# Reordering the opening of a one-core token-mixing, projection and LoRA kernel, and moving its wave generation from GpSimd to ScalarE

## The chip, the cores and the metric

The kernel runs on one core of one Trainium2 chip. The metric is the device time of one execution in microseconds (us). The engines go by short names here as in the profile: PE is TensorE (matrix products and transposes through the identity), DVE is VectorE, ACT is ScalarE, POOL is GpSimd, and SP is the engine whose queue issues nearly all DMAs.

## The reference

What is computed, cut to what matters (L = 1024, H = 128 heads of rows, C = 32, N = 64 states):

```python
K = 2.0 * einsum('chn,hnl->chl', Cc * (exp(dtA) - 1) / A, exp(dtA * ell)).real   # S4D kernel, (32, 128, 1024)
h = K
h = h + (layernorm(h) @ W1.T + b1)                     # W1 is 1024 x 1024
n = layernorm(h)
gates = softmax(n @ Wr.T)                              # 4 experts
lora = sum_e gates_e * 2.0 * (n @ A_e.T) @ Bm_e        # rank 8 each
h = h + (n @ W2.T + b2) + lora                         # W2 is 1024 x 1024
```

## The kernel before, in words

The 4096 rows are worked in 16 tiles t of 8 heads, each in two halves i of 128 rows. One half (t, i) passes through these stages.

- **Waves and S4 product.** `phases` makes the turns of a tile (step times frequency, plus a quarter for the cosine), `round_turns` (DVE, L960 and L963) leaves the fraction, `sines` (ACT, L666, between two table loads) takes the sine, `decays` the exponential, and `make_u` (DVE, L970) multiplies the two. `make_m` (DVE, three passes, L994 and L997) makes the other factor from x, which PE turned (`turn_x`) and ACT copied (`copy_x`). `s4(t, i)` is 64 small PE products into the two banks `ps_a`.
- **First layer norm and G1.** `keep_h` (DVE, L1003) stores h and its sum, `square_1` and `rstd_guess` (ACT), `normalise_1` (DVE, L1028). The result is split in two f16 parts, `high_1` (ACT, L692) and `low_1` (DVE, L1034). `turn_x1` has SP transpose both by DMA into `x1`. `attn(t, i)` is the product G1 with W1: for each of 8 blocks k three partial products (hi by hi, hi by lo, lo by hi) over two halves of the columns, 48 matmuls into the two banks `ps_g1`.
- **Second layer norm and G2.** `keep_h2` (DVE, L1042) reads `ps_g1`, then `square_2`, `normalise_2`, `high_2`, `low_2`, `turn_x2` in the same manner. `project` makes the LoRA and gate products, `ffn_part` is the product G2 with W2 into `ps_g2`, `gate_begin`, `gate_exp`, `gate_end` make the gates, `turn_lora` and `copy_lora` turn them, `ffn_end` adds the LoRA part, and `finish` writes the result for `store`.

In the loop the order on PE is `turn_x(t+1)`, and then twice `s4(after)`, `attn(t, i)`, `project`, `ffn_part`, `turn_lora`, `ffn_part`, `ffn_end` of the half before. The order of the work is written out by hand on each engine, with semaphores between them; an engine runs its list strictly in order. ACT starts an iteration with `copy_x(t+1)`. POOL makes in each iteration one product for the phases and one for the exponents, each over 128x1024 elements (`wave`, L843), when `round_turns` and `make_u` of the tile before are done; ACT then adds the quarter (`quarters`, L657) and takes the exponential (L662) with one instruction each.

**Before the loop** the weights must be made ready. Both are scaled by a power of two, found from a bound on their norm: PE multiplies each 128-row block with itself (`square_attn`, `square_ffn`, L449; `square_lora_a` adds the LoRA weights), DVE reads the diagonal (`weight_norms`, L1113, L1119), POOL takes the largest over the partitions, and DVE makes the scale (`split_scales`, L1126 to L1135). W1, blocks 0 to 7, is turned on PE (`turn_weight`, L473) and split by ACT (`attn_hi`, L710) and DVE (`attn_lo`, L1142) out of PSUM. W2, blocks 8 to 15, is split first (`ffn_hi` L721, `ffn_lo` L1150) and then transposed by DMA (`turn_weights` on SP). `high` parts are announced on `s_whi`, `low` parts on `s_wlo`, counters whose order the tuple `SPLITS` holds.

The prologue on PE interleaves all this with the first halves: `attn(0, 0)` by column halves as the blocks of W1 come, `s4(0, 1)`, `attn(0, 1)`, `turn_lora_b`, `s4(1, 0)`, `project(0, 0)`, G2 of (0, 0). G2 there waits at once for all eight blocks of W2 (`s_wf`).

Of the kernel before, what the change touches and what calls it, by code (L numbers as in the profile page):

```python
# [15 lines left out]
P = 128  # L16
# [6 lines left out]
HT = 8  # L23
# [23 lines left out]
SPLITS = (0, 1, 2, 3, 8, 4, 9, 5, 6, 10, 7, 11, 12, 13, 14, 15)  # L47
# [13 lines left out]
def program(nc, x, log_dt, B, inv_A_real, A_imag, attn_w, attn_b, ffn_w, ffn_b, lora_a, lora_b,  # L61
            gate_w, out):
    with ExitStack() as ctx:
# [26 lines left out]
        norms = sb("norms", [P, 4])  # L90
# [35 lines left out]
        x2_tok = stage[:, KB - 2, :]  # L126
# [4 lines left out]
        def x1_part(part):  # L131
            return x1[:, :].bitcast(F16).rearrange("p (s k t) -> p s k t", s=2, k=KB)[:, part, :, :]
# [28 lines left out]
        s_norm = sem("weight_squares_summed")  # L161
        s_diag = sem("weight_norms_read")
# [3 lines left out]
        s_wf, s_wf_0 = sem("ffn_weight_transposed"), sem("first_ffn_rows_transposed")  # L166
# [13 lines left out]
        s_phase = sem("phase_ready")  # L180
        s_arg = sem("exponent_ready")
# [130 lines left out]
        def _(sp):  # L312
# [92 lines left out]
        def _(pe):  # L405
# [82 lines left out]
            def ffn_part(t, i, ks):  # L488
# [93 lines left out]
            pe.wait_ge(s_wf, 32 * (KB - 1))  # L582
            ffn_part(0, 0, range(0, 6))
# [712 lines left out]
```

## Time and profile before

| | |
|---|---|
| median of 3 runs | 863.32 us (862.34 to 863.69) |
| time of the profiled execution | 863.63 us |
| its span, first to last instruction | 861.8 us |
| PE busy | 822.8 us (95% of the span) |
| DVE busy | 602.3 us (70%) |
| ACT busy | 323.6 us (38%) |
| POOL busy | 67.2 us (8%) |
| mean granted TensorE clock | 0.99 |

The span lies 1.8 us under the time of the same execution. The page shows one execution; the queries used here give, for a stretch of it, the instructions in order of time (start, duration, and in square brackets the idle time before them and what ended it), the waits summed by who waited for whom, and groups of instructions with their mean duration.

### The profile page before, as it was taken

What the parts mean: (1) busy time and instruction counts of PE and PEld (TensorE: products, weight loads), DVE (VectorE), ACT (ScalarE), POOL (GpSimd) and SP (SyncE); (2) the same over time, 40 slices, a digit from 0 to 9 for tenths busy, and PEclk for the clock granted to TensorE, in tenths of its full rate; (3) what the DMA queues carried; (4) which work ended last, traced back from release to release, by engine and by line L of the source; (5) the groups of instructions that cost most, each with busy time, mean ns of one, the idle gap of its engine ahead of it and who ended that gap; (6) DMA issues with size and microseconds to landing.
All of it is one profiled execution on the core that took longest, in us unless ns stands there. A gap on an engine that the chain in (4) does not pass through costs nothing.

```text
span 861.8 us, 15882 instructions
## 1 busy us (share of the span) xinstructions
PE 822.8 (95%) x6162; PEld 437.5 (51%) x6162; DVE 602.3 (70%) x1150; ACT 323.6 (38%) x543; POOL 67.2 (8%) x38
## 2 busy tenths in 40 slices
PE   6976979999999999999999999999999999999998
PEld 6863434545545454545545454545545454545543
DVE  6867877587777767687777767687776757687433
ACT  4645544252524334252424334252424334252210
POOL 0001002020200102020200102020200202000000
PEclk9988999999999999999999999999999999999999
DMA  8536643223332333223323333223323333223323
GB/s 293 154 75 112 115 84 77 58 65 73 73 68 66 73 84 75 50 67 72 79 61 73 73 81 73 52 61 72 85 56 79 73 79 66 62 53 69 75 50 73
DMA packets 175267, 68.47 MB, mean 79 GB/s; under 512 B 160456, under 2 KB 168776, under 8 KB 175248
## 3 DMA queue, kind: packets, MB, share of 16 engines
q1 hardware_dynamic: 175152, 68.09, 36.0%
q8 instruction: 11, 0.18, 0.1%
q10 hardware_dynamic: 96, 0.13, 0.0%
q14 instruction: 8, 0.07, 0.0%
HBM read 13.67 MB, written 16.78 MB: 35 GB/s over the span
## 4 chain that ended last, share of the span: by engine, by line
PE 61%; DVE 18%; ACT 10%; issue 10%; DMA 0%; DVEq 0%; SPq 0%; ACTq 0%
PE ps_g L495 24%; PE ps_g L435 21%; PE ps_a L427 7%; DVE y L1028 2%; DVE m_im L994 2%; DVE h_tok L1042 2%; ACT junk L678 2%; DVE h_tok L1003 2%; ACT L666 2%; ACT x_tok L692 2%; PE ps_g L506 2%; ACT turn_u L666 2%; PE ps_g L619 1%; DVE stat L1014 1%; PE ps_x L449 1%
## 5 line engine op out<-in xcount | busy, mean ns | idle before, releaser
L435 PE MATMUL ps_g<-wa_hi,x 128*128 128x512 f16 x1024 | 272.7, 382 | 8.5 <-DVE wa_lo L1142 4.8
L495 PE MATMUL ps_g<-wf_hi,x 128*128 128x512 f16 x992 | 264.9, 380 | 0.0
L435 PEld LDWEIGHTS ps_g<-wa_hi,x 128*128 128x128 f16 x1024 | 98.3, 98 | 130.2 <-issue 9.4
L435 PE MATMUL ps_g<-wa_lo,x 128*128 128x512 f16 x512 | 155.0, 382 | 0.0
L495 PEld LDWEIGHTS ps_g<-wf_hi,x 128*128 128x128 f16 x992 | 95.5, 98 | 105.0 <-issue 1.3
L495 PE MATMUL ps_g<-wf_lo,x 128*128 128x512 f16 x496 | 148.0, 380 | 0.0
L672 ACT ACTIVATE junk<-ps_a,stat 128x1024 bf16<-128x1024 f32 x32 | 35.7, 1115 | 150.9 <-DVE stat L1006 150.9
L1104 DVE SCALAR_TENSOR_TENSOR result<-ps_g,unscale,h_tok 128x1024 f32<-128x1024 f32 x31 | 39.8, 1284 | 68.5 <-PE ps_g L506 68.5
L843 POOL TENSOR_TENSOR phase<-z_turn,steps_b 128x1024 f32<-128x1024 f32 x14 | 38.1, 2719 | 576.6 <-DVE turn_u L963 576.6
L435 PEld LDWEIGHTS ps_g<-wa_lo,x 128*128 128x128 f16 x512 | 50.4, 98 | 61.0 <-issue 1.8
L495 PEld LDWEIGHTS ps_g<-wf_lo,x 128*128 128x128 f16 x496 | 48.6, 98 | 59.2 <-issue 1.1
L678 ACT ACTIVATE junk<-h_tok,stat 128x1024 bf16<-128x1024 f32 x32 | 36.7, 1148 | 106.0 <-DVE stat L1046 106.0
L692 ACT ACTIVATE x_tok<-y 128x1024 f16<-128x1024 f32 x32 | 33.8, 1057 | 100.0 <-DVE y L1028 100.0
L427 PE MATMUL ps_a<-turn_u,m 128*32 128x128 f32 x2048 | 64.2, 279 | 5.3 <-DVE wa_lo L1142 4.2
L427 PEld LDWEIGHTS ps_a<-turn_u,m 128*32 128x32 f32 x2048 | 55.3, 112 | 13.6 <-issue 5.9
L1003 DVE SCALAR_TENSOR_TENSOR h_tok<-ps_a,bias_bc 128x1024 f32<-128x1024 f32 x32 | 39.2, 1224 | 25.2 <-PE ps_a L427 25.2
L1042 DVE SCALAR_TENSOR_TENSOR h_tok<-ps_g,unscale,h_tok 128x1024 f32<-128x1024 f32 x32 | 40.9, 1278 | 20.7 <-PE ps_g L435 20.7
L1034 DVE TENSOR_TENSOR x_tok<-y,x_tok 128x1024 f16<-128x1024 f32 x32 | 39.1, 1222 | 21.5 <-ACT x_tok L692 21.5
L698 ACT ACTIVATE stage<-xn 128x1024 f16<-128x1024 f32 x32 | 33.8, 1057 | 47.6 <-DVE xn L1053 47.6
L1059 DVE TENSOR_TENSOR stage<-xn,stage 128x1024 f16<-128x1024 f32 x32 | 39.2, 1225 | 12.7 <-ACT stage L698 12.6
L1028 DVE TENSOR_SCALAR y<-ps_a,stat 128x1024 f32<-128x1024 f32 x32 | 43.0, 1343 | 1.2
L994 DVE TENSOR_TENSOR m<-x_t,q 128x1024 f32<-128x1024 f32 x32 | 40.7, 1271 | 1.6
(194 smaller groups left out, 832.8 us busy)
## 6 DMA issues: line engine op xcount, KB each, us to landing
out<-result SPq DMA_DIRECT2D x124, 128.0 KB, 2.1
x_raw<-in_x SPq DMA_DIRECT2D x64, 64.0 KB
stage<-in_L_ffn_W SPq DMA_DIRECT2D x8, 512.0 KB, 9.9
h_tok<-in_L_attn_weight SPq DMA_DIRECT2D x2, 512.0 KB, 4.6
x<-in_L_attn_weight SPq DMA_DIRECT2D x2, 512.0 KB, 7.0
result<-in_L_attn_weight SPq DMA_DIRECT2D x2, 512.0 KB, 8.3
x<-x_tok SPq DMA_TRANSPOSE x64, 3.2
x<-stage SPq DMA_TRANSPOSE x64, 3.2
```

Of the source, the lines that this page charges most:

```text
L427: mm = pe.matmul(ps_a[q * C:(q + 1) * C, a // 4, (a % 4) * P:(a % 4 + 1) * P], m[:, i, q, a * C:(a + 1) * C], u[:, HS * i + q, :], start=T ...
L435: mm = pe.matmul(ps_g1[:, o, :], x1_part(part)[:, k, :], ws[:, k, o * HALF:(o + 1) * HALF], start=k == 0 and part == 0 and ws is wa_hi, st ...
L495: pe.matmul(ps_g2[:, o, :], xs[:, k, :], ws[:, k, o * HALF:(o + 1) * HALF], start=k == 0 and xs is x2_hi and ws is wf_hi, stop=False)
L678: act.activation(junk[:, :], h2_tok[:, i, :], ACT.Square, bias=stat_2[:, 1:2], accum_out=stat_2[:, 2:3]).then_inc(s_ssq2, 1)
L692: act.activation(by_token(x1_tok[:, :], 0), y[:, :], ACT.Copy).then_inc(s_hi1, 1)
L994: dve.tensor_tensor(dst.rearrange("p h (a c) -> p h a c", a=KB), c, f, ALU.mult)\
L1003: dve.scalar_tensor_tensor(out=h_tok[:, i, :], in0=whole(ps_a), scalar=1.0, in1=bias_bc[:, :], op0=ALU.mult, op1=ALU.add, accum_out=stat_1 ...
L1028: dve.tensor_scalar(y[:, :], whole(ps_a), stat_1[:, 1:2], stat_1[:, 7:8], ALU.add, ALU.mult).then_inc(s_xn1, 1)
L1034: dve.tensor_tensor(by_token(x1_tok[:, :], 1), y[:, :], by_token(x1_tok[:, :], 0), ALU.subtract)\
L1042: dve.scalar_tensor_tensor(out=h2_tok[:, i, :], in0=whole(ps_g1), scalar=unscale[:, 0:1], in1=h_tok[:, i, :], op0=ALU.mult, op1=ALU.add, a ...
L1059: dve.tensor_tensor(by_token(x2_tok, 1), xn[:, :], by_token(x2_tok, 0), ALU.subtract)\
L1104: dve.scalar_tensor_tensor(out=result[:, i, :], in0=whole(ps_g2), scalar=unscale[:, 1:2], in1=h2_tok[:, i, :], op0=ALU.mult, op1=ALU.add). ...
```

## The change

The sums of squares of W2's blocks 12 to 15 are taken by ACT, one row sum for each (`square_rows`, the bound is then a maximum over the diagonal of the other four blocks and these four columns of `norms`), and no longer by PE. W1's splits come ahead of most of W2's: `attn_lo(2, 3)` stands before the second `weight_norms`, and the orders of high and low parts differ (`SPLITS`, `LOWS`). Piece 4 of W1 is turned into `ps_g2` instead of `ps_a`. The product G1 of half (0, 1) goes into `ps_g2`, with its x in `x2[:, 1]`, so that it needs neither `ps_g1` nor `x1`; `turn_lora_b` goes into `ps_g1`. G2 of (0, 0) is made by column halves, the first of which waits for blocks 8 to 11 only, with `s4(1, 0)` inside it. Copies 9 and 10 of W2's splits lie in `result`, and `x2_tok` in `stage[:, 0]`. In all tiles the waves are made by ACT: `phases` and `decays` are 8 instructions each over 128x128 elements, with the scale addressed by a register in the loop, at the top of the iteration; POOL's `wave`, ACT's `quarters` and the one-instruction `decays` are gone.

The diff, cut to its core:

```diff
-SPLITS = (0, 1, 2, 3, 8, 4, 9, 5, 6, 10, 7, 11, 12, 13, 14, 15)
+SPLITS = (0, 1, 2, 3, 4, 5, 8, 6, 9, 7, 10, 11, 12, 13, 14, 15)
+LOWS = (0, 1, 2, 3, 4, 5, 8, 6, 7, 9, 10, 11, 12, 13, 14, 15)
-        norms = sb("norms", [P, 4])
+        norms = sb("norms", [P, 8])
-        x2_tok = stage[:, KB - 2, :]
+        x2_tok = stage[:, 0, :]
-            ps = (ps_g1, ps_g2, ps_g1, ps_g2, ps_a, None, ps_g2, None)[n]
+            ps = (ps_g1, ps_g2, ps_g1, ps_g2, ps_g2, None, ps_g2, None)[n]
...
@@ sync
             def turn_x1(t, i):
-                at_least(sp, s_g1, 2 * t + i)
+                first = (t, i) == (0, 1)
+                if first:
+                    sp.wait_ge(s_wt, 5)
+                else:
+                    at_least(sp, s_g1, 2 * t + i)
...
             turn_x1(0, 0)
             load_x(1)
-            turn_weights(KB, KB + 3)
+            turn_weights(KB, KB + 1)
             sp.wait_ge(s_wt, KB)
             load_lora_a(wg_rows, s_wg)
-            turn_weights(KB + 3, KB + 4)
             turn_x1(0, 1)
-            turn_weights(KB + 4, 2 * KB)
+            turn_weights(KB + 1, KB + 5)
             turn_x2(0, 0)
+            turn_weights(KB + 5, 2 * KB)
             load_x(2)
@@ tensor
             s4(0, 0)
-            square_ffn(KB + 2, 2 * KB)
+            square_ffn(KB + 2, KB + 4)
             square_lora_a()
-            pe.wait_ge(s_wlo, split_done(0))
+            pe.wait_ge(s_wlo, low_done(0))
             turn_weight(2)
-            pe.wait_ge(s_wlo, split_done(1))
+            pe.wait_ge(s_wlo, low_done(1))
             turn_weight(3)
-            pe.wait_ge(s_xn1, 1)
+            pe.wait_ge(s_wlo, low_done(3))
             turn_weight(4)
             pe.wait_ge(s_diag, 2)
             turn_weight(5)
+            pe.wait_ge(s_wlo, low_done(4))
+            turn_weight(6)
             pe.wait_ge(s_x1, 32)
-            pe.wait_ge(s_wlo, split_done(3))
-            attn_part(0, 0, range(0, 1), (0,))
-            turn_weight(6)
-            attn_part(0, 0, range(1, 5), (0,))
-            pe.wait_ge(s_wlo, split_done(4))
+            attn_part(0, 0, range(0, 4), (0,))
             s4(0, 1)
-            attn_part(0, 0, range(5, KB), (0,))
-            pe.wait_ge(s_wlo, split_done(5))
+            pe.wait_ge(s_wlo, low_done(5))
             turn_weight(7)
-            pe.wait_ge(s_wlo, split_done(7))
+            attn_part(0, 0, range(4, KB), (0,))
+            pe.wait_ge(s_wlo, low_done(7))
             attn_part(0, 0, range(KB), (1,)).then_inc(s_g1, 1)
             turn_x(1)
             turn_lora_a()
-            attn(0, 1)
+            pe.wait_ge(s_x1, 64)
+            attn_part(0, 1, range(0, 6), ps=ps_g2)
             turn_lora_b()
-            s4(1, 0)
+            attn_part(0, 1, range(6, KB), ps=ps_g2).then_inc(s_g1, 1)
...
             project(0, 0)
             pe.wait_ge(s_lb_sb, 2)
             pe.wait_ge(s_wf_0, 32)
-            pe.wait_ge(s_wf, 32 * (KB - 1))
-            ffn_part(0, 0, range(0, 6))
+            pe.wait_ge(s_wf[0], 96)
+            pe.wait_ge(s_h2, 2)
+            ffn_part(0, 0, range(0, 3), (0,))
+            s4(1, 0)
+            ffn_part(0, 0, range(3, KB), (0,))
+            pe.wait_ge(s_wf[1], 128)
+            ffn_part(0, 0, range(0, 3), (1,))
             turn_lora(0, 0)
-            ffn_part(0, 0, range(6, KB))
+            ffn_part(0, 0, range(3, KB), (1,))
             ffn_end(0, 0)
@@ scalar
             def phases(T):
+                at_least(act, s_frac, T)
                 for k in range(HT):
                     a = act.activation(phase[:, k, :], steps_b[:, :], ACT.Identity,
-                                       scale=z_turn[:, T * HT + k:T * HT + k + 1], bias=quarter[:, :])
+                                       scale=z_turn[:, bass.ds(T * HT + k, 1)], bias=quarter[:, :])
+            def decays(T):
+                act.wait_ge(s_u, T)
                 for k in range(HT):
+                    a = act.activation(decay[:, k, :], steps_b[:, :], ACT.Exp,
+                                       scale=z_re[:, bass.ds(T * HT + k, 1)])
+            def square_rows(*blocks):
+                for n in blocks:
+                    act.wait_ge(s_wload[n], 16)
+                    at_least(act, s_rows, n - KB - KB // 2)
+                    act.activation(junk[:, :], raw_block(n), ACT.Square,
+                                   accum_out=norms[:, n - KB:n - KB + 1]).then_inc(s_rows, 1)
             square_1(0, 0)
             rstd_guess(0, 0, stat_1, s_ssq1, s_log1, s_y1)
+            square_rows(12, 13)
             high_1(0, 0)
             attn_hi(2, 3)
+            square_rows(14, 15)
+            attn_hi(4, 5)
             ffn_hi(8)
-            attn_hi(4)
+            attn_hi(6)
             ffn_hi(9)
-            attn_hi(5, 6)
-            act.wait_ge(s_frac, 1)
-            phases(1)
+            attn_hi(7)
+            act.wait_ge(s_rows, KB // 2)
             square_1(0, 1)
...
             with act.Fori(1, TILES - 1) as t:
+                phases(t + 1)
+                decays(t + 1)
                 copy_x(t + 1)
@@ gpsimd
-            waves(2)
-            with pool.Fori(1, TILES - 2) as t:
-                waves(t + 2)
@@ vector
             low_1(0, 0)
+            attn_lo(2, 3)
             dve.wait_ge(s_lo1, 1)
             weight_norms(1, [ps_x[:, :], ps_p[:, :]])
-            attn_lo(2, 3)
+            make_first_u(1)
             split_scales(1)
+            attn_lo(4)
+            make_m(0, 1)
+            attn_lo(5)
             ffn_lo(8)
-            make_first_u(1)
-            make_m(0, 1)
-            attn_lo(4)
-            ffn_lo(9)
-            attn_lo(5)
+            attn_lo(6)
             keep_h(0, 1)
-            attn_lo(6)
-            ffn_lo(10)
             attn_lo(7)
             normalise_1(0, 1)
-            ffn_lo(11)
+            ffn_lo(9)
             low_1(0, 1)
-            round_turns(1)
-            ffn_lo(12)
-            dve.wait_ge(s_wf_0, 32)
-            keep_h2(0, 0)
+            ffn_lo(10, 11, 12)
             split_lora_b()
...
-            ffn_lo(13, 14)
+            ffn_lo(13)
+            keep_h2(0, 0)
+            ffn_lo(14)
+            round_turns(1)
             normalise_2(0, 0)
             ffn_lo(15)
             low_2(0, 0)
...
+            make_m(1, 0)
+            dve.wait_ge(s_wf_0, 32)
+            keep_h2(0, 1, ps_g2)
+            make_u(1)
+            gate_begin(0, 0)
+            gate_end(0, 0)
+            keep_h(1, 0)
+            normalise_2(0, 1)
+            normalise_1(1, 0)
+            copy_lora(0, 0)
+            low_1(1, 0)
             make_m(1, 1)
-            keep_h(1, 0)
-            normalise_1(1, 0)
-            low_1(1, 0)
-            gate_begin(0, 0)
-            keep_h2(0, 1)
-            gate_end(0, 0)
-            normalise_2(0, 1)
             low_2(0, 1)
-            copy_lora(0, 0)
```

## Rows read from the trace of the kernel before

**Rows 1.** The page: PE's granted clock in 40 slices of the span.

```profile
PEclk9988999999999999999999999999999999999999
```

**Rows 2.** Waits of PE, 0 to 121 us: sum, times, longest.

```profile
PE ps_p L500 <- DVE lora_split L1091: 4.8, 1, 4.8
PE ps_g L435 <- DVE wa_lo L1142: 4.8, 2, 3.6
PE ps_a L427 <- DVE wa_lo L1142: 4.2, 1, 4.2
PE ps_g L435 <- DMA x<-x_tok: 3.7, 1, 3.7
```

**Rows 3.** Waits of PE, 120 to 862 us.

```profile
PE ps_p L500 <- DVE lora_split L1091: 6.4, 13, 0.5
```

**Rows 4.** PE in order of time, prologue.

```profile
35.91 1.16 PE L449 MATMUL ps_x<-stage 128*128 128x128 f32 x8
...
46.82 1.16 PE L449 MATMUL ps_x<-x 36*128 36x128 f32 x8
...
62.26 3.64 PE L427 MATMUL ps_a<-turn_u,m 128*32 128x128 f32 x64 [4.23 <-DVE wa_lo L1142]
...
84.76 1.03 PE L435 MATMUL ps_g<-wa_hi,x 128*128 128x512 f16 x2 [3.65 <-DMA x<-x_tok]
...
121.09 1.95 PE L427 MATMUL ps_a<-turn_u,m 128*32 128x128 f32 x64
```

**Rows 5.** Groups on DVE, 34 to 121 us: busy, mean ns.

```profile
L1150 DVE SCALAR_TENSOR_TENSOR stage<-stage,scale 128x1024 f16<-128x1024 f32 x6 | 7.6, 1280 | 4.8 <-ACT stage L721 4.8
...
L997 DVE TENSOR_TENSOR m<-m,m_im 128x1024 f32<-128x1024 f32 x3 | 3.7, 1225 | 0.1
```

**Rows 6.** ACT in order of time, prologue.

```profile
42.19 1.06 ACT L692 ACTIVATE x_tok<-y 128x1024 f16<-128x1024 f32 x1 [2.80 <-DVE y L1028]
...
59.57 3.19 ACT L637 ACTIVATE phase<-steps_b,quarter,z_turn 128x128 f32<-128x128 f32 x8
...
81.03 2.43 ACT L651 ACTIVATE decay<-steps_b,z_re 128x128 f32<-128x128 f32 x8
...
84.19 1.15 ACT L678 ACTIVATE junk<-h_tok,stat 128x1024 bf16<-128x1024 f32 x1 [0.73 <-DVE stat L1046]
```

**Rows 7.** DVE in order of time, prologue.

```profile
54.16 0.14 DVE L1135 TENSOR_SCALAR unscale<-power 128x1 f32<-128x1 f32 x1
...
84.07 0.59 DVE L1165 TENSOR_SCALAR params<-params 128x256 f32<-128x256 f32 x1
...
85.88 0.22 DVE L1214 TENSOR_SCALAR lora_split<-ones,scale 128x2 fp32r<-128x2 f32 x1
...
103.64 1.22 DVE L1003 SCALAR_TENSOR_TENSOR h_tok<-ps_a,bias_bc 128x1024 f32<-128x1024 f32 x1
...
110.35 1.23 DVE L1034 TENSOR_TENSOR x_tok<-y,x_tok 128x1024 f16<-128x1024 f32 x1 [1.12 <-ACT x_tok L692]
```

**Rows 8.** SP's queue, prologue.

```profile
81.34 1.34 SPq L338 DMA_TRANSPOSE x<-x_tok  x1
```

**Rows 9.** One iteration of the loop: ACT in order of time.

```profile
503.64 1.06 ACT L698 ACTIVATE stage<-xn 128x1024 f16<-128x1024 f32 x1 [1.44 <-DVE xn L1053]
510.45 0.60 ACT L631 ACTIVATE x_t<-ps_x 128x512 f32<-128x512 f32 x1 [5.75 <-PE ps_x L413]
```

**Rows 10.** The same iteration: DVE.

```profile
513.88 1.23 DVE L994 TENSOR_TENSOR m<-x_t,q 128x1024 f32<-128x1024 f32 x1
...
523.27 2.26 DVE L970 TENSOR_TENSOR turn_u<-decay,turn_u 128x1024 f32<-128x1024 f32 x1 [0.58 <-ACT turn_u L666]
525.45 1.27 DVE L1042 SCALAR_TENSOR_TENSOR h_tok<-ps_g,unscale,h_tok 128x1024 f32<-128x1024 f32 x1
```

**Rows 11.** The same iteration: POOL.

```profile
521.74 2.71 POOL L843 TENSOR_TENSOR phase<-z_turn,steps_b 128x1024 f32<-128x1024 f32 x1 [42.79 <-DVE turn_u L963]
```

**Rows 12.** The same iteration: PE.

```profile
531.40 0.32 PE L500 MATMUL ps_p<-ident,lora_split 128*98 128x128 f32 x1 [0.49 <-DVE lora_split L1091]
```

More of the change, by code:

```diff
@@ L429, in s4, with attn_part @@
                 mm.then_inc(s_s4, 1)
-            def attn_part(t, i, ks, halves=(0, 1)):
+            def attn_part(t, i, ks, halves=(0, 1), ps=ps_g1):
                 for k in ks:
@@ L434, in attn_part @@
                         for o in halves:
-                            mm = pe.matmul(ps_g1[:, o, :], x1_part(part)[:, k, :], ws[:, k, o * HALF:(o + 1) * HALF],
+                            mm = pe.matmul(ps[:, o, :], x1_part(part, ps is ps_g2)[:, k, :], ws[:, k, o * HALF:(o + 1) * HALF],
                                            start=k == 0 and part == 0 and ws is wa_hi,
@@ L486, in project, with ffn_part @@
                 mm.then_inc(s_proj, 1)
-            def ffn_part(t, i, ks):
+            def ffn_part(t, i, ks, halves=(0, 1)):
                 if 0 in ks:
@@ L493, in ffn_part @@
                     for xs, ws in ((x2_hi, wf_hi), (x2_hi, wf_lo), (x2_lo, wf_hi)):
-                        for o in range(2):
+                        for o in halves:
                             pe.matmul(ps_g2[:, o, :], xs[:, k, :], ws[:, k, o * HALF:(o + 1) * HALF],
@@ L517, in turn_lora_b @@
                 pe.wait_ge(s_lbn, 3)
+                pe.wait_ge(s_h2, 1)
                 for o in range(2):
                     for j in range(4):
-                        mm = pe.transpose(ps_g2[0:KL, o, j * P:(j + 1) * P], lbn[:, 4 * o + j, :].bitcast(F32),
+                        mm = pe.transpose(ps_g1[0:KL, o, j * P:(j + 1) * P], lbn[:, 4 * o + j, :].bitcast(F32),
                                           ident[:, :])
@@ L772, in _ @@
             ffn_hi(10)
-            attn_hi(7)
             high_1(0, 1)
-            ffn_hi(11, 12)
+            ffn_hi(11, 12, 13)
+            phases(1)
             copy_x(1)
-            second_decays()
+            ffn_hi(14)
             square_2(0, 0)
             rstd_guess(0, 0, stat_2, s_ssq2, s_log2, s_y2)
-            ffn_hi(13, 14, 15)
-            act.wait_ge(s_wlo, split_done(14))
+            ffn_hi(15)
+            act.wait_ge(s_wlo, low_done(8))
             high_2(0, 0)
-            sines(1)
             act.wait_ge(s_wg_t, 1)
@@ L788, in _ @@
                 act.wait_ge(s_lbt, o + 1)
-                act.activation(lb[:, o * HALF:(o + 1) * HALF], ps_g2[0:KL, o, :], ACT.Copy).then_inc(s_lb_sb, 1)
+                act.activation(lb[:, o * HALF:(o + 1) * HALF], ps_g1[0:KL, o, :], ACT.Copy).then_inc(s_lb_sb, 1)
+            decays(1)
+            sines(1)
+            square_2(0, 1)
+            rstd_guess(0, 1, stat_2, s_ssq2, s_log2, s_y2)
+            gate_exp(0, 0)
             square_1(1, 0)
@@ L793, in _ @@
             high_1(1, 0)
-            gate_exp(0, 0)
-            square_2(0, 1)
-            rstd_guess(0, 1, stat_2, s_ssq2, s_log2, s_y2)
             high_2(0, 1)
@@ L1035, in low_1, with keep_h2 @@
                     .then_inc(s_lo1, 1)
-            def keep_h2(t, i):
+            def keep_h2(t, i, ps=ps_g1):
                 j = 2 * t + i
@@ L1041, in keep_h2 @@
                 at_least(dve, s_result, j - 1)
-                dve.scalar_tensor_tensor(out=h2_tok[:, i, :], in0=whole(ps_g1), scalar=unscale[:, 0:1],
+                dve.scalar_tensor_tensor(out=h2_tok[:, i, :], in0=whole(ps), scalar=unscale[:, 0:1],
                                          in1=h_tok[:, i, :], op0=ALU.mult, op1=ALU.add,
@@ L1112, in weight_norms @@
                     blocks = ps.shape[1] // P
+                    norm = 2 * k + j
                     a = dve.scalar_tensor_tensor(out=y[:, cols].rearrange("p (k o) -> p k o", o=P),
@@ L1219, in _ @@
             low_2(0, 0)
-            make_m(1, 0)
-            make_u(1)
             dve.wait_ge(s_wg_hi, 1)
```

71 lines of the change are left out of this document (29 added, 42 removed).

## The prediction

> **What bounds the kernel now.** I read the page first. The granted clock is full nearly everywhere but in the third to sixth slice of 40, all before 130 us [rows 1]. So I asked for PE's waits before and after 120 us. Before it, PE waits for W1's low parts, for the transposed x of half (0, 1), and at the end for the gates [rows 2]; the four kinds sum to 17.5 us, and with the waits of about 1 us it is 20. After it PE waits for one thing only, 13 times about 0.5 us, 6.4 us in all, for `lora_split` [rows 3]. Then I read PE, DVE, ACT and SP in order of time up to the start of `s4(1, 1)` at 121.09 [rows 4], from where on nothing but those short waits holds PE. The change has two sizes to find: how much sooner `s4(1, 1)` starts, and what an iteration of the loop gains or loses.
>
> **The opening, step by step.** Each wait is priced by the chain that now ends last. Full-width DVE passes take 1.23 to 1.28 us and follow each other every 1.2 [rows 5].
>
> 1. *Squares.* Six blocks of W2 take PE from 35.91 to 46.82, 1.82 each [rows 4]. Four go: 7.3 us, so the norm's sums end near 41.6 instead of 48.8. They don't set the next step. DVE now does `attn_lo(2, 3)` first, and these need ACT's `attn_hi(2, 3)`, which follow `high_1(0, 0)`. That one ends at 43.25 in any case [rows 6]: the two squares ahead of it (1.15 each and 0.1 for the sum, 2.5 together, by the square of rows 6) fill 2.5 of the 2.80 us in which ACT idles there. So high parts 2 and 3 end at 44.3 and 45.3, low ones at 45.7 and 46.9. The second pair of squares ends at 47.8, under this. Reading the diagonal takes DVE to 48.2, and with the maximum over the partitions the scale stands at 49.7, against 54.3 [rows 7]. That is 4.6 us sooner, not 7.3. If W2's blocks had not landed, ACT's squares would be late; PE read block 12 near 39.6 without a wait, so this costs nothing.
> 2. *DVE sets the pace to the second x.* From 49.7: low 4 (1.25), `make_m(0, 1)` (3 passes, 3.5), low 5 in two pieces (1.4), low 8 and low 6 (2.4) end at 58.2. PE has meanwhile turned pieces 4 to 6, begun G1 at 52 and ended `s4(0, 1)` at 56.5, so `keep_h(0, 1)` starts at 58.2. In the row of before that `s4` began at 62.26 and took 3.64 at half clock [rows 4]. From the start of `keep_h` to the end of `low_1` it takes 7.9 us where nothing comes between (103.64 to 111.58 [rows 7]); lows 7 and 9 fit in its waits. So `low_1(0, 1)` ends at 66.1. Its transpose lands 3.4 us after its issue (81.34, and PE starts at 84.76 [rows 4, 8]): x is there at 69.5, against 84.7. On SP this transpose now stands ahead of those of blocks 9 to 12.
> 3. *G1 of both halves.* PE ends the first by 66.4. The second needs no free `ps_g1`. With 48 matmuls (10.4) and `turn_lora_b` (1.05) it runs from 69.5 to 81.0.
> 4. *DVE again.* Between 66.1 and the end of `keep_h2(0, 1)`, which G2 of (0, 0) needs since it lies in `ps_g2`, DVE has 13 full-width passes (six `ffn_lo`, two `keep_h2`, one of `round_turns`, `low_2`, three of `make_m(1, 0)`), 15.6 us, and short ones: `split_lora_b` to `lora_split` 2.0 (84.07 to 86.10 [rows 7]), the passes of `round_turns` and `normalise_2` on SBUF alone 1.4, statistics and `wg_lo` 1.8. Sum 20.8, so 86.9. x2 of (0, 0), split by 81.6, lands at 85 to 86: the same time. ACT's phases (3.19) and exponentials (2.43 [rows 6]) lie in ACT's gaps here. G2 starts at 87.0.
> 5. *The price of PE's pause.* PE has little to do from 81.0 to 87.0. After the pauses of 4.23 and 3.65 us in rows 4, `s4` took 3.64 instead of 1.95 and the first matmuls of G1 ran at the lower of the two clock levels, 1.2 instead of 2.4 GHz. I take the first 9 matmuls and part of `s4(1, 0)` at half clock: 3.9 plus 2.1 instead of 1.95 plus 1.9. `s4(1, 0)` ends at 93.0. The same holds for the pause from 43.4 to 47.0 (PE waits for low 3): the transposes of pieces 4 and 5 are on the chain of step 2, and I take 0.6 us for it. Its bounds are nothing, and 3 us if the half clock lasts through `s4(0, 1)`.
> 6. *To the loop.* From the end of `s4(1, 0)`: 7.9 to the end of `low_1(1, 0)`, then `make_m(1, 1)` 3.5, on which `s4(1, 1)` waits: 104.5. PE itself is through with G2 (39 more matmuls, 8.4, and 1.4 for the small products) at 102.9. All eight blocks of W2 are needed at 96; SP issues the last at 90, and they land by 95.
>
> With the 0.6 of step 5 `s4(1, 1)` starts at 105.1 instead of 121.09: **16.0 us saved**. Bounds: 102.6 with no half clock anywhere gives 18.5 (the last step then starts at 90.9 and nothing is added); 3 us for the first pause, 2 more for the second, and half a microsecond of wait at each of four handovers give 11.
>
> **The loop.** DVE's `make_u` takes 2.26 us there, while POOL's product of the phases runs (521.74 to 524.45), and `keep_h2` stands right behind it [rows 10, 11]. The same kind of instruction takes 1.23 elsewhere [rows 5]. Without POOL, `make_u` ends 1.03 sooner, `keep_h2` starts as much sooner (its product ended at 522.5), and by the chain `keep_h2`, `square_2`, `normalise_2`, `gate_end` so does `lora_split`. PE's wait of 0.49 [rows 12] goes: **6.4 us saved** over the loop [rows 3]. More is not to be had: the rest of the iteration shows no idle time on PE.
>
> What ACT pays: per tile 3.19 and 2.43 instead of two instructions of about 1.1, so 3.4 more. They stand after `high_2`, which ends at 504.70, and end at 510.3; `copy_x` started at 510.45 after 5.75 idle [rows 9]. So the cover holds to 0.1 us, and behind `copy_x` waits `make_m` at 513.88 [rows 10], 2.8 us later. A register address costs something that no row of ACT shows. From below it is nothing, if it is made ready under the instruction before; from above I take 0.2 us each, the gap ahead of DVE's first register-addressed pass less the usual overlap (513.76 to 513.88 [rows 10], and about 0.1). 16 of them give 3.2 us. The slack is 2.8 and then the 0.54 that `make_u` gives beyond the wait: 3.4. So either end costs nothing, and I take nothing.
>
> The Trainium skill (VectorE: DVE Perf Modes, the section on the TRN2 errata) warns of this: operations out of SBUF pay a fixed time each, so small tiles cost more. The rows agree, 5.62 against 2.2 us for the same elements; it is ACT's time, which has that room. Its cycle formula gives 0.29 us for 128 elements, an estimate from that page: 4.7 for 16, and the sum would be the same by it.
>
> **Sum.** 16.0 + 6.4 = 22.4. The profiled execution took 863.63 us (span 861.8, 1.8 beside it), so 841.2; against the median of 863.32 it is 841 as well. I say 841.3.
>
> **The rivals.**
>
> - *The loop keeps its wait.* ACT's table loads and sine end at 524.5, and if `square_2` or the order of `copy_x` is pushed, the 1.03 us of `make_u` does not reach `lora_split`. For: the slack left is only 0.54. Against: the chain has no other wait of that size. Time: 863.6 - 16.0 = 847.6.
> - *The opening gives only what PE no longer does.* DVE is the bound from 49.7 on, and a wait that I have placed wrong (SP's transposes of eight blocks packed together, landing over 4 us late, or the clock) gives the rest back: 7.3 saved, and the loop's 6.4: 850. Against: the x of (0, 1) comes 15 us sooner by three independent queues.
> - *Slower: register-addressed ACT instructions.* In the loop each of the 16 pays x more. Beyond 0.21 us each, every microsecond reaches PE 14 times: 14 * 16 * (x - 0.21) over a loop without the wait. It decides at x = 0.31, where it eats all 22.4 us. At 0.35 the time is 841.3 + 31 = 873. For: no row of ACT has such an address. Against: DVE's shows 0.2 at most, and those behind the first show none.
> - *No change* would need the opening's gain to be lost before the loop; PE has nothing to wait on for that long.
>
> **How the numbers follow.** Forecast 0.58; loop keeps its wait 0.18; opening gives only 7.3 0.10; better than the sum (no half clock, 838 and below) 0.07; slower 0.05; no change 0.02. The range reaches from 838 (the bound of no half clock, 863.6 - 18.5 - 6.9) to 851 (just over the second rival). Faster by over 0.2% (1.7 us, about what a measurement here can tell from no change) 0.93, same 0.02, slower 0.05.
>
> **What would show each step.** In the profile after: the scale of W2 near 49.7; `low_1(0, 1)` ending near 66 and G1 of (0, 1) starting near 69.5; G2 of (0, 0) near 87 at half clock; `s4(1, 1)` near 105; in the loop `make_u` at 1.22 and no wait of PE for `lora_split`; ACT's 16 instructions in 5.6 us ending by 511 in the iteration of rows 9. The prediction is wrong if PE's waits in the loop grow (then ACT's instructions are over 0.6 us apart), or if DVE idles between 50 and 87, which would mean a wait that I have not seen.

## The result and the profile after

The changed kernel takes 840.09 us (median of 4 runs, 838.85 to 840.41), the one before 862.83 (4 runs): the ratio is 0.9734, 95% interval 0.9718 to 0.9751. The forecast was 841.3, with a range from 838 to 851. The total is right to 1.2 us. Its two terms are less so, and they miss in opposite directions; the experiments below size them. In the group of runs with e1, e2, e9 and e10 one execution of the kernel before took 1365.4 us at a mean granted clock of 0.59, and it is left out of every figure.

The profiled execution took 838.85 us (span 837.0), the lowest of the four. The head of its page, with engines as in the table before, and PE's clock to compare with [rows 1]:

```profile
span 837.0 us, 16105 instructions
## 1 busy us (share of the span) xinstructions
PE 811.0 (97%) x6098; PEld 431.0 (51%) x6098; DVE 586.9 (70%) x1150; ACT 376.6 (45%) x747; POOL 3.0 (0%) x10
...
PEclk9999999999999999999999999999999999999999
```

PE is busy 11.8 us less and DVE 15.4 less; ACT is busy 53.0 us more. PE's waits from 0 to 106 us of the changed kernel, to set beside [rows 2]:

```profile
PE ps_g L487 <- DVE wa_lo L1149: 4.8, 2, 3.3
PE ps_p L497 <- DMA x<-stage: 2.5, 1, 2.5
PE ps_g L449 <- DMA x<-x_tok: 2.2, 1, 2.2
PE ps_a L441 <- DVE m L1001: 2.1, 1, 2.1
...
PE ps_g L509 <- DVE h_tok L1046: 1.1, 1, 1.1
PE ps_g L449 <- DVE wa_lo L1149: 0.8, 1, 0.8
```

The wait of 4.2 for `s4(0, 1)` and the 4.8 for the gates are gone. The marks of the opening, PE in order of time, against [rows 4] (L441 is `s4`, L449 G1, L509 G2):

```profile
47.26 1.97 PE L487 MATMUL ps_g<-ident,x 128*128 128x128 f32 x8 [3.32 <-DVE wa_lo L1149]
...
53.14 0.38 PE L449 MATMUL ps_g<-wa_hi,x 128*128 128x512 f16 x1
...
70.75 0.90 PE L449 MATMUL ps_g<-wa_hi,x 128*128 128x512 f16 x2 [2.17 <-DMA x<-x_tok]
...
88.07 0.59 PE L509 MATMUL ps_g<-wf_hi,x 128*128 128x512 f16 x1 [1.14 <-DVE h_tok L1046]
...
91.74 1.96 PE L441 MATMUL ps_a<-turn_u,m 128*32 128x128 f32 x64
...
105.37 1.95 PE L441 MATMUL ps_a<-turn_u,m 128*32 128x128 f32 x64 [2.11 <-DVE m L1001]
```

And DVE, against [rows 7]: the scale of W2, the end of `low_1(0, 1)`, and `keep_h2(0, 1)`.

```profile
50.11 0.14 DVE L1142 TENSOR_SCALAR unscale<-power 128x1 f32<-128x1 f32 x1
...
66.07 1.22 DVE L1038 TENSOR_TENSOR x_tok<-y,x_tok 128x1024 f16<-128x1024 f32 x1
...
86.64 1.28 DVE L1046 SCALAR_TENSOR_TENSOR h_tok<-ps_g,unscale,h_tok 128x1024 f32<-128x1024 f32 x1
```

Step for step this is the predicted chain, and its marks are at most 1.3 us off: scale 49.7 (here 50.2), end of `low_1(0, 1)` 66.1 (67.3), G1 of (0, 1) 69.5 (70.75), G2 of (0, 0) 87.0 (88.07), `s4(1, 1)` 105.1 (105.37). The end of the second G1, which is not on that chain, came 2.8 us later than forecast (83.85 instead of 81.0): it started later and at the lower clock. PE's half clock shows elsewhere too: piece 4 took 1.97 instead of 1.04 after 3.3 us of pause, and the 9 matmuls from 88.07 took 3.7.

In the loop, one iteration on DVE and ACT, against [rows 9, 10]:

```profile
502.03 1.23 DVE L974 TENSOR_TENSOR turn_u<-decay,turn_u 128x1024 f32<-128x1024 f32 x1 [0.58 <-ACT turn_u L677]
503.17 1.28 DVE L1046 SCALAR_TENSOR_TENSOR h_tok<-ps_g,unscale,h_tok 128x1024 f32<-128x1024 f32 x1
```

```profile
482.39 1.06 ACT L709 ACTIVATE stage<-xn 128x1024 f16<-128x1024 f32 x1 [1.44 <-DVE xn L1057]
483.36 3.17 ACT L657 ACTIVATE phase<-steps_b,quarter,z_turn 128x128 f32<-128x128 f32 x8
486.43 2.43 ACT L671 ACTIVATE decay<-steps_b,z_re 128x128 f32<-128x128 f32 x8
489.21 0.60 ACT L650 ACTIVATE x_t<-ps_x 128x512 f32<-128x512 f32 x1 [0.35 <-PE ps_x L427]
...
530.35 1.06 ACT L709 ACTIVATE stage<-xn 128x1024 f16<-128x1024 f32 x1 [1.44 <-DVE xn L1057]
```

`make_u` is down from 2.26 to 1.23, and PE waits for nothing between 106 and 837 us. ACT's 16 instructions with a register address take as long as those with a fixed one, 3.17 and 2.43 against 3.19 and 2.43 [rows 6]. But the iteration is now 47.96 us (482.39 to 530.35), and before the same mark stood at 503.64 [rows 9] and next at 552.29, 48.65 us later:

```profile
552.29 1.06 ACT L698 ACTIVATE stage<-xn 128x1024 f16<-128x1024 f32 x1 [1.44 <-DVE xn L1053]
```

So an iteration gained 0.69, not the 0.49 of [rows 12]. The wait stood in 13 of the 14 iterations [rows 3], since POOL's loop had one turn fewer than the others, and the last iteration takes 47.5 us in both kernels. 13 times 0.69 is 9.0, not 6.4, and the two profiles agree: from the start of `s4(1, 1)` to the end of the span it is 740.7 us before and 731.6 after, 9.1 less.

### The profile page after: what moved, and what is told of

Read it like the earlier page. It is cut to its first block, busy times and chain, and to the rows that moved or that the text cites. A ratio compares the mean times of both kernels' runs of the same rounds, so it can differ in the third digit from the quotient of the medians.

```text
span 837.0 us, 16105 instructions
## 1 busy us (share of the span) xinstructions
PE 811.0 (97%) x6098; PEld 431.0 (51%) x6098; DVE 586.9 (70%) x1150; ACT 376.6 (45%) x747; POOL 3.0 (0%) x10
## 4 chain that ended last, share of the span: by engine, by line
PE 88%; DVE 5%; issue 3%; ACT 2%; DMA 1%; SPq 0%; POOL 0%; POOLq 0%; ACTq 0%; DVEq 0%
PE ps_g L509 38%; PE ps_g L449 38%; PE ps_a L441 7%; PE ps_g L520 2%; PE ps_g L638 1%; PE ps_p L497 1%; PE ps_g L463 1%; PE ps_x L427 1%; DMA h_tok<-in_L_attn_weight 1%; PE ps_p L499 1%; DVE m L998 0%; DVE m_im L998 0%; PE ps_p L514 0%; ACT phase L657 0%; DVE wa_lo L1149 0%
## 5 line engine op out<-in xcount | busy, mean ns | idle before, releaser
L449 PE MATMUL ps_g<-wa_hi,x 128*128 128x512 f16 x1024 | 271.5, 381 | 2.9 <-DMA x<-x_tok 2.2
L509 PE MATMUL ps_g<-wf_hi,x 128*128 128x512 f16 x992 | 265.7, 381 | 1.1 <-DVE h_tok L1046 1.1
L449 PEld LDWEIGHTS ps_g<-wa_hi,x 128*128 128x128 f16 x1024 | 97.7, 98 | 123.4 <-issue 7.4
L449 PE MATMUL ps_g<-wa_lo,x 128*128 128x512 f16 x512 | 154.4, 381 | 0.0
L509 PEld LDWEIGHTS ps_g<-wf_hi,x 128*128 128x128 f16 x992 | 94.9, 98 | 108.0 <-issue 2.8
L509 PE MATMUL ps_g<-wf_lo,x 128*128 128x512 f16 x496 | 149.6, 381 | 0.0
L449 PEld LDWEIGHTS ps_g<-wa_lo,x 128*128 128x128 f16 x512 | 50.2, 98 | 60.7 <-issue 1.0
L509 PEld LDWEIGHTS ps_g<-wf_lo,x 128*128 128x128 f16 x496 | 48.5, 98 | 58.6 <-issue 0.6
L441 PE MATMUL ps_a<-turn_u,m 128*32 128x128 f32 x2048 | 62.5, 274 | 2.4 <-DVE m L1001 2.1
L441 PEld LDWEIGHTS ps_a<-turn_u,m 128*32 128x32 f32 x2048 | 54.0, 110 | 10.8 <-issue 9.2
L657 ACT ACTIVATE phase<-steps_b,quarter,z_turn 128x128 f32<-128x128 f32 x128 | 50.8, 479 | 0.0
```

The source lines that it names most:

```text
L441: mm = pe.matmul(ps_a[q * C:(q + 1) * C, a // 4, (a % 4) * P:(a % 4 + 1) * P], m[:, i, q, a * C:(a + 1) * C], u[:, HS * i + q, :], start=T ...
L449: mm = pe.matmul(ps[:, o, :], x1_part(part, ps is ps_g2)[:, k, :], ws[:, k, o * HALF:(o + 1) * HALF], start=k == 0 and part == 0 and ws is ...
L509: pe.matmul(ps_g2[:, o, :], xs[:, k, :], ws[:, k, o * HALF:(o + 1) * HALF], start=k == 0 and xs is x2_hi and ws is wf_hi, stop=False)
L657: a = act.activation(phase[:, k, :], steps_b[:, :], ACT.Identity, scale=z_turn[:, bass.ds(T * HT + k, 1)], bias=quarter[:, :])
```

## The experiments

All times are medians of 4 or 5 runs, and each ratio is to the kernel before as it was measured beside that run (862.5 to 862.8 us). A kernel "without" a part is the changed kernel with that part undone. "s4(1, 1)" is its start in the profile.

| kernel | us | ratio to before, 95% interval | s4(1, 1) |
|---|---|---|---|
| before | 862.8 | | 121.09 |
| changed | 840.1 | 0.9718 to 0.9751 | 105.37 |
| e1: changed, waves by POOL | 850.4 | 0.9836 to 0.9871 | 107.29 |
| e2: before, waves by ACT | 853.4 | 0.9869 to 0.9905 | 119.80 |
| e9: changed, idle POOL product at the fractions | 849.7 | 0.9827 to 0.9863 | 105.95 |
| e10: changed, the same product at u | 839.3 | 0.9717 to 0.9754 | 103.94 |
| e3: before, squares by ACT | 857.7 | 0.9928 to 0.9962 | 114.38 |
| e4: changed without the squares by ACT | 846.6 | 0.9797 to 0.9829 | 111.62 |
| e5: changed without G1 in G2's banks | 841.8 | 0.9736 to 0.9768 | 107.56 |
| e6: changed without G2 by halves | 842.8 | 0.9754 to 0.9786 | 109.50 |
| e12: changed without all three | 848.4 | 0.9821 to 0.9854 | 115.05 |
| e7: phases made twice | 839.8 | 0.9716 to 0.9746 | 105.38 |
| e8: phases and exponentials twice | 869.6 | 1.0063 to 1.0094 | 105.60 |
| e11: changed, `keep_h2(0, 1)` first | 838.0 | 0.9700 to 0.9727 | 104.61 |

### The loop: is it POOL's product on DVE's pass?

**e1**, the changed kernel with POOL's `waves`, ACT's `quarters` and the one-instruction exponential as before; **e2**, the reverse, the kernel before with

```diff
             with act.Fori(1, TILES - 1) as t:
+                phases(t + 1)
+                decays(t + 1)
                 copy_x(t + 1)
...
-            waves(2)
-            with pool.Fori(1, TILES - 2) as t:
-                waves(t + 2)
```

> The opening of the changed kernel, the loop of the one before: POOL makes the waves and ACT adds the quarter and takes the exponential with one instruction each. Theory A (POOL's product holds up DVE's make_u by 1.04 us, and this alone makes PE's wait for lora_split): make_u 2.26 us, that wait back 13 times with 0.49 us idle, s4(1, 1) near 105.4, and 9 us over the changed kernel, so 849 (the two profiled spans differ by 24.8, of which 15.7 lie before s4(1, 1)). Rival B (the loop gained nothing of its own, the opening all of it): 840. The 6.4 us of the prediction would make it 846.5.

> The opening of the kernel before, with ACT making the waves of tiles 2 and on. Theory A: s4(1, 1) at 121 as before, no wait of PE in the loop, 9 us less than before, so 854. Rival B: 863. If opening and loop are independent, the gains of this run and of the one with POOL's waves add up to that of the whole change, 22.7.

The loop is worth 10.3 us by the one (850.4 against 840.1) and 9.5 by the other (862.8, the kernel before measured beside it, against 853.4). The opening is then worth 12.5 and 13.3. Rival B is out, and the two are independent to within what the medians can tell: the gains of e1 and e2 add up to 22.0, the whole change gave 22.7. The 9.1 of the profiles lies under both medians; what the lower clock costs one execution and not another is sized below ("Why the prediction was right", item 5).

These two change ACT's order as well. **e9** and **e10** leave it as it is and only give POOL a product that nobody reads:

```diff
+            with pool.Fori(1, TILES - 2) as t:
+                pool.wait_ge(s_frac, t + 2)        # e10: s_u
+                pool.tensor_tensor(spare[:, :].rearrange("p (h l) -> p h l", h=HT),
+                                   z_turn[:, bass.ds((t + 2) * HT, HT)].unsqueeze(2).broadcast_to((P, HT, P)),
+                                   steps_b[:, :].unsqueeze(1).broadcast_to((P, HT, P)), ALU.mult)\
+                    .then_inc(s_phase, 1)
+                pool.wait_ge(s_phase, t)
```

> The changed kernel, and POOL makes in the loop one product more, of the size of the phases, at the moment at which it made them before (when the fractions are ready), into a buffer that nobody reads. Theory A: it delays only make_u, from 1.23 to 2.26 us; PE's wait returns, 849. Rival C (the gain came from ACT's new order, phases and exponentials early in the iteration): 840, no wait.

> The same useless product on POOL, but started when make_u is done, so that it runs beside keep_h2, which reads PSUM and one operand in SBUF. Theory A in its narrow form (only a pass with both operands in SBUF waits for POOL, as the second product of before, which ran beside keep_h2, left that at 1.27 us): keep_h2 stays at 1.28, no wait of PE, 840. Rival D (any work of POOL holds up any DVE pass): keep_h2 takes about 1 us longer, and with 0.4 us of slack PE waits again, 849.

POOL in e9, the two DVE passes beside it, and PE's wait in the loop, which is back:

```profile
508.27 2.63 POOL L871 TENSOR_TENSOR spare<-z_turn,steps_b 128x1024 f32<-128x1024 f32 x1 [46.01 <-DVE turn_u L975]
```

```profile
509.73 2.25 DVE L982 TENSOR_TENSOR turn_u<-decay,turn_u 128x1024 f32<-128x1024 f32 x1 [0.58 <-ACT turn_u L678]
511.91 1.27 DVE L1054 SCALAR_TENSOR_TENSOR h_tok<-ps_g,unscale,h_tok 128x1024 f32<-128x1024 f32 x1
```

```profile
PE ps_p L515 <- DVE lora_split L1103: 6.3, 13, 0.5
```

And in e10, where PE waits for nothing in the loop:

```profile
502.10 1.90 POOL L871 TENSOR_TENSOR spare<-z_turn,steps_b 128x1024 f32<-128x1024 f32 x1 [46.06 <-DVE turn_u L982]
```

```profile
500.62 1.22 DVE L982 TENSOR_TENSOR turn_u<-decay,turn_u 128x1024 f32<-128x1024 f32 x1 [0.58 <-ACT turn_u L678]
501.76 1.28 DVE L1054 SCALAR_TENSOR_TENSOR h_tok<-ps_g,unscale,h_tok 128x1024 f32<-128x1024 f32 x1
```

One product per tile, 2.6 us on an engine that does nothing else, costs 9.6 us when it meets the pass with both operands in SBUF, and nothing when it meets the one that reads PSUM. Rivals C and D are out. The Trainium skill (GPSIMD Engine Reference, Key points) says that GpSimd shares its SBUF interfaces with VectorE and contends with its instructions that have two SBUF inputs; the two runs agree: `make_u` takes 2.25 us beside POOL's product and 1.22 without it, `keep_h2` keeps its 1.28 beside it. The runs tell these two passes apart; that the place of the operands is the reason is the skill's statement, and no run here changes that alone. The waits of PE's weight loads in e9 also tell what a stall costs:

```profile
PEld ps_p L515 <- DVE lora_split L1103: 12.7, 13, 1.0
```

PE's matmuls overlap (0.38 us each by their rows, one every 0.22), so the idle time of 0.49 between two rows leaves out what the last one had still to run when the stall began: 0.38 - 0.22 = 0.16. 0.49 + 0.16 is 0.65, near the 0.69 of the iteration; the weight loads show 0.98, which is too much. Laid side by side, the rows of PE give the rest. Before, then the changed kernel, at the same place of the iteration:

```profile
530.32 0.59 PE L495 MATMUL ps_g<-wf_hi,x 128*128 128x512 f16 x2
...
531.56 0.59 PE L495 MATMUL ps_g<-wf_hi,x 128*128 128x512 f16 x2
```

```profile
509.07 0.59 PE L509 MATMUL ps_g<-wf_hi,x 128*128 128x512 f16 x2
509.51 0.27 PE L514 MATMUL ps_p<-ident,lora_split 128*98 128x128 f32 x1
509.62 0.59 PE L509 MATMUL ps_g<-wf_hi,x 128*128 128x512 f16 x2
```

From the start of the pair before the gates' product to the start of the pair behind it, it is 1.24 us before (530.32 to 531.56, with the 531.40 of [rows 12] between) and 0.55 after: 0.69.

### How much cover do ACT's waves have?

**e7** and **e8** make the phases, or both, twice; the extra instructions write rows of `stage` that nobody reads.

```diff
-                for k in range(HT):
-                    a = act.activation(phase[:, k, :], steps_b[:, :], ACT.Identity,
+                for k, dst in [(0, phase)] + [(k, again[:, 0, :, :]) for k in range(extra)]\
+                        + [(k, phase) for k in range(1, HT)]:
+                    a = act.activation(dst[:, k, :], steps_b[:, :], ACT.Identity,
```

> The changed kernel with ACT making the phases twice in each iteration (8 more instructions, 3.1 us, into a buffer that nobody reads). Theory (the cover of ACT's waves has 2.8 us before make_m and about 0.4 behind it): copy_x comes at 491.9 instead of 489.2 in the iteration shown, make_m still at 492.6: no change, 840. Rival (ACT's waves have no cover left, as they end 0.35 us ahead of copy_x): 14 times 2.7 us, 878.

> The changed kernel with phases and exponentials both made twice (16 more, 5.5 us). Theory: copy_x ends at 495.0, 2.4 us after DVE could begin make_m; the whole chain to lora_split moves by 2.4, of which 0.4 is slack: 14 times 2.0, so 868. Rival (ACT has 50% idle time, it hides all of it): 840.

839.8 and 869.6, as forecast by the theory in both. 3.1 us more are free although ACT's waves ended only 0.35 us ahead of `copy_x`; 5.5 us more cost 29.5. In e8 DVE stands before `make_m` for `copy_x`, and PE before the gates:

```profile
513.34 1.23 DVE L1001 TENSOR_TENSOR m<-x_t,q 128x1024 f32<-128x1024 f32 x1 [2.50 <-ACT x_t L651]
```

```profile
PE ps_p L515 <- DVE lora_split L1098: 26.1, 14, 1.9
```

### The opening: which part brings what?

**e3** is the kernel before with the squares of blocks 12 to 15 on ACT (12, 13 ahead of `high_1(0, 0)`, 14, 15 behind it). **e4** takes them away from the changed kernel:

```diff
-            square_ffn(KB + 2, KB + 4)
+            square_ffn(KB + 2, 2 * KB)
...
-            square_rows(12, 13)
...
-            square_rows(14, 15)
```

> The kernel before with one part of the change alone: ACT takes the squares of blocks 12 to 15 in its two pauses beside high_1(0, 0), PE those of 8 to 11. Theory (DVE's chain sets the pace): the norm's sums end at 41.6, DVE reads the diagonal right after low_1(0, 0), at 44.5 instead of 49.0, and the chain behind it shifts by 4 to 4.5 us: 858.8. Rival (what PE no longer does is the gain): 7.3 us, 855.5. Rival (another wait takes its place): 863.

> The changed kernel with all squares back on PE. Theory: in the changed order the norms stand behind attn_lo(2, 3), which stand behind the turning of blocks 2 and 3, which stands behind the squares on PE; so all of it comes 7 us later and the opening loses nearly the full 7.3: s4(1, 1) near 112, 847. Rival (the reordering is what counts, the squares hide in the gaps): under 2 us lost, 841.

e3: 4.8 us less than its kernel before (862.5), between the two expectations and nearer to the chain's 4 to 4.5. Its scale of W2 is ready here:

```profile
48.43 0.14 DVE L1148 TENSOR_SCALAR unscale<-power 128x1 f32<-128x1 f32 x1
```

Counted from the start of `low_1(0, 0)` (43.28 before, 42.12 in e3) this step begins 4.6 us sooner. In e3's profile `s4(0, 1)` also runs at full clock, 1.95 us instead of 3.64, and `keep_h(0, 1)`, which waited for it before, comes another 1.3 us sooner. e4: 6.5 us more, where the theory said 7; there the scale is ready at 55.9 instead of 50.2, 6.7 us later if both are counted from the start of `low_1(0, 0)` (last small step of the scale in e4):

```profile
55.72 0.14 DVE L1137 TENSOR_SCALAR unscale<-power 128x1 f32<-128x1 f32 x1
```

**e5** puts G1 of (0, 1) back into its own banks (and its x into `x1`, `turn_lora_b` into G2's), **e6** makes G2 of (0, 0) in one piece:

```diff
-            attn_part(0, 1, range(0, 6), ps=ps_g2)
+            pe.wait_ge(s_h2, 1)
+            attn_part(0, 1, range(0, 6))
...
-            ffn_part(0, 0, range(0, 3), (0,))
-            s4(1, 0)
-            ffn_part(0, 0, range(3, KB), (0,))
-            pe.wait_ge(s_wf[1], 128)
-            ffn_part(0, 0, range(0, 3), (1,))
+            s4(1, 0)
+            pe.wait_ge(s_wf[1], 128)
+            pe.wait_ge(s_h2, 2)
+            ffn_part(0, 0, range(0, 6))
```

> The changed kernel with the product G1 of (0, 1) back in its own banks and its x back in x1, turn_lora_b in the banks of G2. G1 of (0, 1) then waits for keep_h2(0, 0), which ends at 75.1 (it began at 70.75): 4.4 us later. Theory: most of that was slack, because keep_h2(0, 1) waited on DVE until 86.6 anyway; the product now ends at 88.5, keep_h2(0, 1) at 89.8, but G2 need not wait for it and starts as x2 is there: under 2 us lost, 840 to 842. Rival: the 4.4 us are lost in full, 844.5.

> The changed kernel with the first G2 in one piece, behind s4(1, 0), and waiting for all of W2. s4(1, 0) can start at 89.3 and end by 91 to 93; G2 starts when the last block lands, at 94.6, and ends at 105.6 instead of 102.6; s4(1, 1) then follows at 106.2 instead of 105.4. Theory: 1 us lost, 841; with half clock after the pause 2.5, 842.5. Rival (the halves hide the whole landing of W2): 5 us or more.

e5 loses 1.7 us, e6 2.7; the theory had under 2, and 1 or with half clock 2.5. In e5 the second G1 does start 3.8 us later, after a wait of 6.6 for `keep_h2(0, 0)`:

```profile
74.58 1.01 PE L446 MATMUL ps_g<-wa_hi,x 128*128 128x512 f16 x2 [6.64 <-DVE h_tok L1042]
```

but less than half of that reaches the loop. In e6 PE pauses on both sides of `s4(1, 0)` (2.6 and 2.0 us). The granted clock is 0.95 from 86 to 88, in the first pause, and at its lower level of 1.2 GHz (0.50) from 88 to 96, through `s4(1, 0)` and the second pause. Windows of 4 us: length, busy times of PE, PEld, DVE, ACT and POOL, then the clock, DMA share and GB/s:

```profile
88.00:92.00 4.00, 2.92 (x56) 2.96 (x60) 2.34 (x9) 2.54 (x7) 0.00 (x0) 0.50 1.39 186
92.00:96.00 4.00, 2.01 (x20) 0.75 (x12) 2.85 (x8) 1.64 (x4) 0.00 (x0) 0.50 0.46 105
96.00:100.00 4.00, 4.00 (x16) 1.56 (x14) 2.23 (x6) 1.65 (x3) 0.00 (x0) 0.75 0.11 35
```

**e12** undoes all three, squares, banks and halves, and keeps the order:

> The changed kernel without three parts of its opening: the squares all on PE, the second G1 in its own banks, the first G2 in one piece for all of W2. What is left of the opening is the order of the work (W1's splits first) on PE, ACT, DVE and SP; the waves are made by ACT. Undone one at a time the three parts cost 6.5, 1.7 and 2.7 us. Theory (independent parts): 840.1 + 10.9 = 851, and against the kernel with the old opening and the new loop (853.4) the order alone is worth 2.5 us. Rival (the parts cover for each other: the second G1 waits for keep_h2(0, 0) and then nothing is gained by it): the cost of all three is less than the sum, 848. Rival (the order without the early norm is worse than the old one): 854 or more.

848.4: the three together are worth 8.3 us, not the 10.9 that they cost one by one. The first rival holds (848), they cover for each other; the single runs of e12 spread from 847.6 to 850.3, so the difference of 2.6 is known to a microsecond or so. Against e2 (853.4), which has the old opening and the same loop, what is left is worth 5 us: the order, together with the buffers that it needs, which no run separates. So the opening's 13 us are about 8 for the three parts and 5 for the order.

### A further step

**e11** places one DVE pass differently:

```diff
-            make_m(1, 0)
             dve.wait_ge(s_wf_0, 32)
             keep_h2(0, 1, ps_g2)
+            make_m(1, 0)
```

> The changed kernel with keep_h2(0, 1) ahead of make_m(1, 0) on DVE. Its product ends at 84.0, so it ends at 85.4 instead of 87.9, and G2 of (0, 0) starts when x2 is there and projected, at 86.8 instead of 88.07. Theory: all behind moves by 1.2 us, s4(1, 1) at 104.2, 839, the fastest kernel of the study. Rival (s4(1, 0) then waits for make_u, which ends at 90.1): nothing gained, 840.

838.03 us (5 runs, 836.62 to 839.08), the fastest of the study, 2.1 under the changed kernel's median. The intervals of the two ratios overlap, so that it is faster than the changed kernel is likely, not shown. The forecast of 1.2 us is not shown either: counted from the start of `low_1(0, 0)`, `s4(1, 1)` starts after 61.4 us, against 61.8 in the changed kernel, and the places at lower clock differ between the two profiles. In its trace PE no longer waits for `keep_h2(0, 1)`; G2 starts as soon as x2 has been projected, and the pause before it is x2's:

```profile
PE ps_p L497 <- DMA x<-stage: 4.2, 1, 4.2
```

## Why the prediction was right, and where its terms were off

1. **Squares, step 1.** Right in mechanism: 7.3 us less on PE made the scale 4.1 us earlier (54.3 to 50.2), and e3 gave 4.8, not 7.3. What it did not see is that the same squares are worth more in the new order, 6.5 (e4), since there the norms stand behind the turning of blocks 2 and 3.
2. **DVE sets the pace, steps 2 and 4.** Right: the chain added up from durations of before hit every mark on it within 1.3 us. Most of the difference stood after step 2: `keep_h(0, 1)` began at 59.31, not 58.2. The changed trace shows DVE busy with hardly a gap from 50.9 to 92.0.
3. **Banks, step 3.** The prediction let the second G1 start 15 us sooner, as its x comes sooner and no bank holds it up. e5 sizes the two: without the free banks it starts 3.8 us later, of which 1.7 reach the total; the rest comes with the x.
4. **Half clock, step 5.** Right at 88: 3.7 us for 9 matmuls, 3.9 forecast. The step took part of `s4(1, 0)` at half clock too; it ran in 1.96 there, and in 2.27 to 2.89 in e1, e7 and e9. What the prediction left out is the pause before `s4(1, 1)`, which it had (1.6 us, measured 2.1) without a price for the clock. In the profiles of e1, e7, e8 and e9, which share this opening, `s4(1, 1)` takes 2.7 to 3.5 us instead of 1.95:

```profile
105.38 3.32 PE L442 MATMUL ps_a<-turn_u,m 128*32 128x128 f32 x64 [2.13 <-DVE m L1003]
```

   (this one of e7). From this start to the end of the span e7 takes 733.2 us and the changed kernel, whose profiled run kept full clock here, 731.6. That makes its one profile better by 1.6 us in this place. Elsewhere it can fall the other way: G1 of (0, 1) started at half clock in the changed kernel (70.75, 0.53 of full in the stretch from 70.7 to 74) and at full clock in e7 and e9.
5. **The opening's sum** was 16.0, and the profiles of the two kernels say 15.7. By medians it is 12.5 to 13.3, within the stated bounds of 11 and 18.5. The marks of an execution move by up to 1.6 us with the first loads (`low_1(0, 0)` starts between 42.1 and 43.8 in the 14 profiles), so they are best counted from there. `s4(1, 1)` then starts after 77.8 us before and 61.8 in the changed kernel: 16.0, as forecast. In e1, e7, e8 and e9, with the same opening, it starts after 61.8 to 63.9 and then costs 0.9 to 1.6 more at the lower clock, which leaves a gain of 13.0 to 14.4, nearer to the medians. Only e10, with 16.2, was spared like the profile of the changed kernel. So the forecast took up to 3 us too little for the half clock of most executions. The lower bound of 11 does not follow from its own terms: 2.4 more for the first pause, 2 for the second and 2 for the handovers, taken from 16.0, leave 9.6.
6. **The loop** was the mis-sized term: 6.4 forecast, 9.1 measured in the profiles and 9.5 to 10.3 by medians. The mechanism is shown by e9 and e10. The size was read from PE's idle time between matmul rows, 0.49 in each of 13 iterations; the iteration itself shrank by 0.69. The term had no upper bound for this.
7. **ACT's cover.** Forecast 2.8 us before `make_m` and 0.54 behind, against which 3.2 were weighed. e7 hides 3.1, e8 exceeds it by 2 us an iteration. The register addresses, the slower rival, cost nothing that the rows show: the x of that rival is nothing by them, and it would have decided at 0.31. The 16 instructions take 5.6 us, as forecast from the rows, and not the 4.7 of the estimate beside it.
8. **The rivals.** "The loop keeps its wait" is out (e1). "The opening gives only what PE no longer does", 7.3, is out: by medians it gave about 13. That the forecast total came so near owes something to chance: by medians the opening gave 3 us less and the loop 3 us more. One reading needs a note: the clock is short of full in the third to sixth slice, as the prediction says, but [rows 1] shows it for the third and fourth only; windows of the same trace give 0.90, 0.82, 0.97 and 0.92 for the four.

## What to carry to other kernels

When a wait shows in the trace as 0.5 us of idle time on PE, measure the period of the loop around it and not the idle time: here the stall cost 40% more. An engine with 8% of busy time can still set the pace, if one of its instructions meets the wrong pass of another; moving its work to an engine that is busier (ACT, 38% to 45%) paid off because the new work stands where 3 us of cover lie ahead of the next reader. In a prologue written out by hand, follow the engine that has no gaps (here DVE) and ask for each removed piece of work where on that engine's list its result is first read: that position, not the duration removed, gives the gain.

## What the runs showed of the hardware that was not expected

- POOL's product and DVE's pass do not slow each other evenly. In e10, beside a pass that reads PSUM, the product takes 1.90 us; in e9, where it meets `low_1` and then `make_u`, 2.63, and `low_1` keeps its 1.22 while `make_u` gets 1.0 us more. It looks as if the one that holds the access finishes first and the other waits; no run tests this further. The kernel before has a second such meeting, in its opening, with another DVE pass that reads two operands in SBUF (`make_m`, 1.22 elsewhere) and starts after POOL's product:

```profile
98.36 1.89 POOL L843 TENSOR_TENSOR decay<-z_re,steps_b 128x1024 f32<-128x1024 f32 x1 [13.84 <-DVE turn_u L970]
```

```profile
98.62 2.71 DVE L994 TENSOR_TENSOR m<-x_t,q 128x1024 f32<-128x1024 f32 x1
```

- A pause of 2.1 us before `s4(1, 1)` was followed by half clock in some executions of one and the same opening (e1, e7, e8, e9) and not in others (changed, e10, e11), so its price is 0 or 0.9 to 1.6 us by execution. The pause before G1 of (0, 1) was followed by half clock in the changed kernel, e1, e8 and e10, where it was 2.2 us long, and not in e7, e9 and e11, where it was 1.8 or 1.9; before `s4(1, 1)` it was 2.1 in all seven, so that the length of the pause alone does not decide.
- Eight ACT instructions over 128x128 elements whose scale is addressed through a register take 3.17 us, those with a fixed address 3.19.
